# Second attention: the fourth output tile of a step is held to the next step in steps 28 and 29 too

## The reference, cut to what matters

```
x = x + l1_attention(layernorm(x), ctx)     # 32 query heads, 8 key/value heads, head size 128,
                                            # q and k rms-normed per head, softmax, times v, times Wo
x = x + gated_ffn(layernorm(x))             # logits = x @ centroids.T, softmax over 64 clusters,
                                            # rows and columns kept by a threshold, dense = x @ W.T + bias
```

## Time and profile before

| what | value |
|---|---|
| median of 3 runs | 1494.99 us (1494.46 to 1495.66) |
| the profiled execution | 1495.35 us, its span 1493.4 us |
| PE busy | 1459.9 us, 98% of the span |
| DVE busy | 1123.8 us, 75% |
| ACT busy | 792.1 us, 53% |
| POOL busy | 709.4 us, 48% |
| mean granted PE clock | 0.996 of full speed |

### The profile page before, as it was taken

One profiled execution on the slowest core, in us unless ns is written; L12 is line 12 of the kernel. 1 busy time (PEld: TensorE's weight loads), 2 busy tenths in 40 slices (PEclk: granted clock), 3 DMA queues, 4 the chain that ended last, 5 costly groups with the idle time before them and its releaser, 6 DMA issues.

```text
span 1493.4 us, 27786 instructions
## 1 busy us (share of the span) xinstructions
PE 1459.9 (98%) x9949; PEld 852.9 (57%) x9949; DVE 1123.8 (75%) x2180; ACT 792.1 (53%) x3201; POOL 709.4 (48%) x668
## 2 busy tenths in 40 slices
PE   8999999999999889999999999999999999999998
PEld 7888645555554445556555555655555565555554
DVE  5887777778877788776776776776677677677868
ACT  6688731211123675555646645654754664565663
POOL 6678875554665454243334424333442433343553
PEclk9999999999999999999999999999999999999999
DMA  5734335442444575644543553554455345344623
GB/s 195 249 133 157 117 82 117 109 74 42 75 82 74 118 152 84 125 93 70 104 97 59 105 92 68 96 87 86 85 88 97 79 83 106 54 64 70 105 48 113
DMA packets 358937, 146.89 MB, mean 98 GB/s; under 512 B 342304, under 2 KB 342688, under 8 KB 356112
## 3 DMA queue, kind: packets, MB, share of 16 engines
q1 hardware_dynamic: 357504, 137.77, 45.5%
q10 hardware_dynamic: 1296, 7.34, 1.5%
HBM read 58.02 MB, written 4.19 MB: 42 GB/s over the span
## 4 chain that ended last, share of the span: by engine, by line
PE 51%; DVE 6%; ACT 5%; POOL 3%; DMA 2%; issue 1%; SPq 0%; DVEq 0%; POOLq 0%; ACTq 0%
PE bank L72 16%; PE bank L73 16%; PE bank L74 16%; PE bank L2621 2%; ACT a_prob L1942 2%; DMA a_kT_lo<-a_kn_lo 2%; POOL a_qrs L1820 1%; ACT a_oT_lo L1919 1%; DVE a_oT_lo L2231 1%; ACT a_qr_hi L1916 1%; DVE a_qve L2170 1%; DVE x_res L2155 1%; POOL a_prob L1803 1%; DVE a_kn L2186 1%; DVE x_res L2318 1%
## 5 line engine op out<-in xcount | busy, mean ns | idle before, releaser
L1942 ACT ACTIVATE a_prob<-a_prob,a_nmx 128x64 f32<-128x64 f32 x512 | 170.2, 334 | 251.6 <-DVE a_nmx L2207 251.6
L1803 POOL TENSOR_TENSOR a_prob<-a_prob,a_mask 128x512 f32<-128x512 f32 x64 | 79.9, 1268 | 276.8 <-DVE a_prob L2201 276.8
L72 PE MATMUL bank<-w,xT_hi 128*128 128x448 f16 (+1 forms) x512 | 188.2, 368 | 3.1 <-DVE h L1313 2.0
L74 PE MATMUL bank<-w,xT_hi 128*128 128x448 f16 (+1 forms) x512 | 188.0, 367 | 0.0
L73 PE MATMUL bank<-w,xT_lo 128*128 128x448 f16 (+1 forms) x512 | 188.0, 367 | 0.0
L1820 POOL TENSOR_TENSOR a_qrs<-a_qve,neg_half 128x8 f32<-128x8 f32 x64 | 104.1, 1647 | 146.6 <-DVE a_qve L2170 146.3
L1239 ACT CAST f_h_hi<-h 128x448 f16<-128x448 f32 x64 | 35.6, 563 | 209.8 <-DVE h L1313 209.7
L2155 DVE SCALAR_TENSOR_TENSOR x_res<-bank,a_oinv,x_res 128x512 f32<-128x512 f32 x128 | 95.5, 746 | 64.1 <-PE bank L74 64.0
L2160 DVE SCALAR_TENSOR_TENSOR a_qr_lo<-bank,a_qr_hi 128x512 f16<-128x512 f32 x128 | 87.8, 687 | 46.5 <-ACT a_oT_lo L1919 27.4
L1809 POOL TENSOR_TENSOR a_p_hi<-a_prob,a_rden 128x512 f16<-128x512 f32 x64 | 69.4, 1085 | 104.5 <-DVE a_rden L2215 104.5
L1177 POOL TENSOR_TENSOR f_h_lo<-h,f_h_hi 128x448 f16<-128x448 f32 x64 | 72.7, 1140 | 91.5 <-ACT f_h_hi L1239 91.5
(11 more groups left out here) (366 smaller groups left out, 4407.3 us busy)
## 6 DMA issues: line engine op xcount, KB each, us to landing
shared<-in_l_wq SPq DMA_DIRECT2D x8, 1024.0 KB, 4.8
shared<-in_l_wo SPq DMA_DIRECT2D x8, 1024.0 KB, 5.1
shared<-in_w ACTq DMA_DIRECT2D x8, 896.0 KB, 4.6
craw<-in_w SPq DMA_DIRECT2D x11, 512.0 KB, 3.7
a_wide<-in_l_ctxT SPq DMA_DIRECT2D x16, 256.0 KB, 3.7
x_res<-in_x SPq DMA_DIRECT2D x16, 256.0 KB, 4.4
shared<-in_ctx SPq DMA_DIRECT2D x16, 256.0 KB, 4.2
shared<-in_l_wkv SPq DMA_DIRECT2D x8, 512.0 KB, 4.2
```

Source lines behind the costliest of these rows:

```text
L72: pe.matmul(out, a_hi, b_hi, start=first, stop=False)
L74: return pe.matmul(out, a_hi, b_lo, start=False, stop=last)
L1803: pool.tensor_tensor(blocks(prob[u][:, :]), blocks(prob[u][:, :]), mask[:, :].unsqueeze(1).broadcast_to([P, NB, S]), ALU.add).then_inc(s_m ...
L1942: ins = act.activation(pt, pt, ACT.Exp, bias=nmx[:, col:col + 1], accum_out=den[:, col:col + 1])
```

## The change

`holds` is true for two more steps, 28 and 29 (`last - 1` is 30, against 28 before). Step 30's fourth tile stays in step 30. With it:

- PE leaves the fourth tile out at the end of steps 28 and 29 and makes it in steps 29 and 30, and steps 29 and 30 get the held order.
- DVE runs `held_tail` in steps 29 and 30. The statistic of the fourth tile of the previous chunk, and the aggregation behind it, go from ahead of `denominators(i, 1)` to behind the held addition, ahead of `outputs(i, 1)`. `gated_spread` stays in step 28 alone; `gated_largest(0)` and `split_centroids` are put into `held_tail`.
- POOL makes the root and the shift of the row statistics behind the query and key roots, not ahead of them.
- ACT's fourth query tile of steps 30 and 31 writes its scratch beside `kn_hi`, as in all held steps, and `outputs(i, 1)` on ACT waits for the held tile.

```diff
--- before.py
+++ after.py
@@ -1659,7 +1659,7 @@
         hi_done = lambda n, t: (n * TPC + t) * 2 + 1
         squares_done = lambda n, t: (n * TPC + t) * 2 + 2
         lo_done = lambda n, t: n * (TPC + 1) + t + (0 if n else 1)
-        holds = lambda i: 0 <= i < (KVH - 1) * NCH
+        holds = lambda i: 0 <= i < last - 1
         out_hi_done = lambda i: (i + 1) * (TPC + 1) + TPC
         kv_banks = [bank[2], bank[3]]
         prep_banks = [bank[2], bank[3], bank[0], bank[1]]
@@ -1838,11 +1838,11 @@
                 normalise(i, 1)
                 if fresh and c == 0:
                     prep.pool_rstd(pool, p0 + 3)
-                if not ahead and c >= 1:
-                    prep.pool_rstd(pool, pf + c - 1)
                 if holds(i - 1):
                     query_roots(i + 1)
                     key_roots(i + 1)
+                    if not ahead and c >= 1:
+                        prep.pool_rstd(pool, pf + c - 1)
                 else:
                     key_roots(i + 1)
                     query_roots(i + 1)
@@ -2357,8 +2357,6 @@
                     weight_powers(g + 1)
                 if not ahead and c == 0:
                     gated_largest_weights()
-                if not ahead and c >= 1:
-                    gated_stats(c - 1, range(3, TPC))
                 denominators(i, 1)
                 if ahead and c == 1 and not fresh:
                     spread_weights(g + 1)
@@ -2445,11 +2443,13 @@
                 values(i + 1, 1, (c + 1) % 2)
                 key_squares((c + 1) % NCH, i + 1)
                 output_hi(i)
-                if not ahead:
+                if not ahead and c == 0:
                     gated_spread()
                 outputs(i, 0)
                 keys(i + 1)
                 add_out((c - 1) % NCH, i - 1, 3)
+                if not ahead and c >= 1:
+                    gated_stats(c - 1, range(3, TPC))
                 outputs(i, 1)
                 keys_lo(i + 1)
                 add_out(c, i, 0)
@@ -2461,11 +2461,15 @@
                     largest_o(dve, m, r, g + 1)
                     weight_powers(g + 1)
                 add_out(c, i, 1)
+                if not ahead and c == 2:
+                    gated_largest(0)
                 if not ahead:
                     gated_stats(c, range(1, 2))
                 add_out(c, i, 2)
                 if not ahead:
                     gated_stats(c, range(2, 3))
+                if not ahead and c == 1:
+                    split_centroids()
                 if not holds(i):
                     add_out(c, i, 3)
                 if fresh and c == 1:
```

## The result

| | before | after |
|---|---|---|
| median of 13 runs each | 1494.99 us (1491.62 to 1497.92) | 1497.22 us (1494.95 to 1499.59) |
| the profiled execution | 1495.35 us | 1496.1 us |
| its span | 1493.4 us | 1494.0 us |
| first scores matmul of step 28 / 29 / 30 / 31 | 1330.30 / 1361.77 / 1391.20 / 1423.85 | 1329.08 / 1357.96 / 1389.50 / 1424.48 |
| from step 28's scores to step 31's | 93.55 us | 95.40 us |

The ratio is 1.0016, with a 95% interval of 1.0008 to 1.0023: slower, but by less than the 0.2% that the prediction named as what a measurement can tell. It forecast 1496.5 us (1494.3 to 1498.6).

What follows compares the result with a forecast made beforehand. PE's work bounds the kernel, with 2.65 us at most to regain; step 30's wait end is set by a chain over other engines. Step 31 starting 1.5 us later makes the span 1494.9 and the median 1496.5 us, range 1494.3 to 1498.6.

Steps and rivals of the forecast that it cites:

- The core: Step 30: PE's wait for the low query tile ends at nearly the same moment, 1403.8, with one more tile behind it.
- the sum: Step 30, PE's keys to step 31: 19.73 plus tile 2.59, less order 0.56, less low-keys wait 0.2, is 21.56 us.
- The size: Step 31 starts at 1425.4 against 1423.85: +1.5 us.
- the start of the normalisation: ACT normalises chunk 0's rows at 1385.77, behind statistics and POOL's root and shift, where it did at 1386.05.
- an unknown of up to 0.5: POOL's root may take up to 0.5 us longer when DVE works beside it.
- SP's transfer of the low keys: Before step 30's scores: no PE wait counted for it; step 30 starts at about 1389.5, one tile after step 29's wait.
- Step 29's wait for the add: PE's third output tile in step 29 waits for DVE's add of tile 0 to free its bank: 1.1 us.
- The low keys' wait in step 30: PE, ready at 1418.35, waits for low keys done at 1418.7: about 0.4 us where it waited 0.6.
- The last step: Nothing is moved there; its length stays unchanged, the last mask beginning at 1427.1 after low halves end at 1426.5.
- Rival 3: Last step: the 0.6 us margin goes, `rows_lo` holds the last mask, up to 1 us slip: 1497.5 us; chance 0.08.
- Rival 1, the clock: Step 30's 2.5 us wait lowers PE's granted clock, from about 2 us of idle time: 1497.6 us; chance 0.20.
- Rival 2, the gain: Waits are covered and PE takes back the 2.65 us of steps 29 and 30: 1492.3 us; chance 0.12.

Runs made afterwards that it cites:

- hold29: Kernel after, but only step 29's fourth tile is held (made in step 30) and step 28 makes its own: 1496.73 us, ratio 1.0010 to the kernel before.
- early: Kernel after with the keys of steps 30 and 31 put behind DVE's held add and row statistics: 1494.78 us, ratio 1.0005 to the kernel before.
- masks: Kernel after with two of chunk 0's four low-half tiles behind step 30's masks on POOL, and `split_centroids` between DVE's denominators: 1494.26 us, ratio 1.0001.
- stats_late: Kernel after with the fourth row statistic and aggregation moved behind the add of tile 0 in steps 29 and 30: 1500.78 us, ratio 1.0034.
- before_masks: Kernel before with two low-half tiles of chunk 0 behind step 30's masks and `split_centroids` between DVE's denominators: 1494.5 us, ratio 1.0002.
- bias_later: Kernel after with SP's bias row load moved from behind step 30's key transposes to behind step 31's: 1496.6 us, ratio 1.0009 to the kernel before.

## Why the prediction was right

**The core held, and part of it is luck.** "The wait ends at nearly the same moment as before, and the work that the hold puts behind it is one tile more": on the time axis of before, PE's keys and values in step 30 start at 1402.87 + 1.22 = 1404.09 against 1404.12. From there to step 31 it takes 1424.48 - 1402.87 = 21.61 us; the sum said 21.56. The prediction placed the new start of the chain rightly, from the statistics, but it never asked what had set the old one, and that was the high keys on ACT. That the two starts coincide is an accident of this kernel. hold29 alone has the loss. early and masks, which shorten the chain or take the masks out of it, give the loss back; stats_late, which lengthens it, makes it larger.

**The size was low by 0.35 us** (+1.5 forecast for the stage, 1.85 measured). The term is the start of the normalisation. The keys of step 29 (1381.14 on the axis of before, 1381.22 forecast) and the end of the statistics (1384.34, 1384.37 forecast) were placed well. Root and shift were taken from the earlier trace rows at 1.37 us and took 1384.71 - 1383.12 = 1.59. POOL's L111 lasted 0.42 us, beside DVE's low keys (1384.23 to 1384.98), and 0.20 in the earlier trace rows and in early, where DVE read a bank at that time. The prediction had this as an unknown of up to 0.5.

**A step that failed: SP's transfer of the low keys.** The prediction let PE start step 30's scores right behind the last output tile. It named the low keys' delay behind the statistics, but counted neither this delay nor their transfer for PE. They were done at 1384.23 + 0.75 = 1384.98; with the 2.5 us that the transfer had taken before it would have been there in time, but it took 4.4, and PE waited 0.96 us. It cost nothing in the stage because it came out of the next wait: that for the queries was forecast at 2.5 us and cost 1.59 (1.43 in brackets). Step 30 started later, and the chain did not. stats_late shows the same from the other side.

**Step 29's wait for the add** was forecast at 1.1 us, from the 1.33 of statistics ahead of it, and cost 1.16 (1.00 in brackets). **The low keys' wait in step 30** was forecast at 0.4 and cost 0.48 (0.32 in brackets).

**The last step** kept its length (69.52 us against 69.55). The margin of its last mask, forecast at 0.6 us, was 0.35. Rival 3 did not come.

**Rival 1, the clock,** did not come in this kernel. Its mechanism was shown at 5.47 us of idle time; the point "from about 2 us" was set too low for this place, as 2.04 us left the clock alone. Between 2.04 and 5.47 it stays open.

**Rival 2, the gain,** needed a normalisation at about 1383.2, 2.6 us earlier. ACT was free for it at 1382.70 on that axis, but the held add ended at 1382.92 there, and its statistic and the root came behind it: ACT stood idle for 3.31 us. That this group would stand in the way is what the prediction had right. masks shows the gain's other way: let the masks not wait for the normalisation. Then the hold comes out 0.55 us ahead of not holding (93.37 against 93.92) and 0.18 ahead of the kernel before, but not the 2.65 us that the rival hoped for, since the waits of step 29 remain (0.98 and 0.86 us in brackets).

## What to carry to other kernels

Work that is moved past a wait pays only if the wait moves with it. Where the wait's end is fixed by a chain over other engines, taking work from ahead of it lengthens the wait, and putting it behind lengthens the kernel by nearly its whole length (here a tile of 2.59 us, less what the new order gave back). So ask first what fixes the end, before and after the change, for it need not be the same thing; place that chain's steps on the new time axis, and shorten the chain before the order on PE is improved; after the shift, look for the next wait of the same length, as before_masks found it in the probabilities.

## What the runs showed of the hardware

**POOL and DVE take turns.** A POOL tile of 128x512 took 3.21 us beside a DVE instruction of 128x2048 (`split_gated`), and 1.15 when it started ahead of it; a DVE instruction of 128x8 took 1.12 us beside POOL's tile, and 0.16 without it. The ends coincide to within 0.03 us. This agrees with the Trainium skill, "SBUF — State Buffer", section "Who interferes with whom": POOL and DVE share a pair of ports, a DVE instruction with two inputs in SBUF contends with a POOL instruction that reads SBUF, and so can a `tensor_scalar` in a mode that uses both of DVE's port pairs; there whoever issues first has the shared pair for its whole instruction and the other is blocked. `split_gated` has two inputs in SBUF; whether the 128x8 instruction, a `tensor_scalar`, ran in such a mode the profile doesn't say. The small end of the same effect may be the 0.22 us by which root and shift were longer than forecast.

**The same transposing transfer can be released 0.5 or 2.2 us after its last byte moved** (hold29 and bias_later). Over all kernels here the low keys of steps 29 to 31 took 2.4 to 4.4 us from issue to landing. The cause is open.

**Idle time of 1.43 and 2.04 us ahead of the same matmul left PE's granted clock at 1.00; 5.47 us brought it to 0.50,** and 2.8 us were lost in the next stretch.
